# Tile 0's layer 0 on unsplit weights, between the turns of W0, in a three-layer CIN kernel

## The reference

```python
x_vec = input                                   # (512, 64, 16): batch b, fields f, embedding d
for W, b in params:                             # three layers, 128 outputs each
    z = jnp.einsum('bhd,bfd->bhfd', x_vec, input)
    z = z.reshape(B, h * f, d)                  # h*f = 4096, then 8192, 8192
    x_vec = jnp.einsum('oc,bcd->bod', W, z) + b[None, :, None]
    outs.append(x_vec.sum(axis=2))
return jnp.concatenate(outs, axis=1)            # (512, 384)
```

## Time and profile before

| | us |
|---|---|
| runs (3) | 1109.91, 1110.55, 1111.24 |
| median | 1110.55 |
| profiled execution | 1111.36 |
| its span, first to last instruction | 1109.6 |
| TensorE busy with matmuls | 1078.9 (97%) |
| VectorE busy | 863.8 (78%) |
| Pool busy | 862.1 (78%) |
| ScalarE busy | 713.5 (64%) |

### The profile page before, as it was taken

One profiled execution on the slowest core, in us unless ns is written; L12 is line 12 of the kernel. 1 busy time (PEld: TensorE's weight loads), 2 busy tenths in 40 slices (PEclk: granted clock), 3 DMA queues, 4 the chain that ended last, 5 costly groups with the idle time before them and its releaser, 6 DMA issues.

```text
span 1109.6 us, 17740 instructions
## 1 busy us (share of the span) xinstructions
PE 1078.9 (97%) x4781; PEld 808.4 (73%) x4781; DVE 863.8 (78%) x2529; ACT 713.5 (64%) x2428; POOL 862.1 (78%) x727
## 2 busy tenths in 40 slices
PE   6889999999999999999999999999999999999997
PEld 5767677777778777777778777777777877777776
DVE  5665888889894788988885698888887588888981
ACT  2566767767673676767673676766766476676771
POOL 2457897989984799897976779797988579798560
PEclk8999999999999999999999999999999999999998
DMA  7743333223241332324332142333232232321000
GB/s 280 196 101 96 74 92 79 77 55 96 50 101 39 66 84 54 97 65 86 84 67 58 45 87 82 70 93 74 77 68 64 63 69 77 79 77 41 1 23 8
DMA packets 108325, 85.87 MB, mean 77 GB/s; under 512 B 71040, under 2 KB 73824, under 8 KB 108096
## 3 DMA queue, kind: packets, MB, share of 16 engines
q1 hardware_dynamic: 106832, 78.17, 28.5%
q10 hardware_dynamic: 1392, 6.55, 1.9%
HBM read 14.75 MB, written 0.79 MB: 14 GB/s over the span
## 4 chain that ended last, share of the span: by engine, by line
PE 85%; DVE 6%; ACT 5%; issue 2%; DMA 1%; POOL 1%; ACTq 0%; DVEq 0%
PE y L881 57%; PE l L901 11%; PE l L881 7%; PE xt L992 5%; PE l2p L1004 3%; DVE acc L740 3%; ACT prod L638 2%; ACT y L627 2%; DVE acc L725 1%; DMA gram<-in_L_rec_W_dram 1%; DVE gram L824 1%; PE l L951 1%; PE l2p L981 1%; ACT x1h L536 1%; DVE bd L696 0%
## 5 line engine op out<-in xcount | busy, mean ns | idle before, releaser
L740 DVE SCALAR_TENSOR_TENSOR acc<-y,x0t,acc 128x128 f32<-128x128 f32 x1792 | 493.2, 340 | 62.6 <-PE y L881 58.2
L638 ACT ACTIVATE prod<-y,x0t 128x128 f32<-128x128 f32 x1280 | 367.7, 380 | 221.7 <-PE y L881 215.3
L881 PE MATMUL y<-w1h,x1h 128*128 128x512 f32 x1024 | 469.1, 458 | 3.9 <-DVE acc L740 3.7
L881 PE MATMUL y<-w1h,x1l 128*128 128x512 f32 x1024 | 402.7, 393 | 0.0
L881 PE MATMUL y<-w1l,x1h 128*128 128x512 f32 x1024 | 401.8, 392 | 0.0
L435 POOL TENSOR_TENSOR z<-z,xg 128x512 f32<-128x512 f32 (+2 forms) x272 | 372.2, 1373 | 24.4 <-DMA z<-xg 24.4
L445 POOL TENSOR_TENSOR pacc<-pacc,prod 128x512 f32<-128x512 f32 x192 | 253.1, 1318 | 137.2 <-ACT prod L638 137.2
L881 PEld LDWEIGHTS y<-w1h,x1h 128*128 128x128 f32 x1024 | 193.5, 189 | 108.4 <-issue 40.6
L627 ACT ACTIVATE y<-y,x0t 128x128 f32<-128x128 f32 x768 | 215.2, 349 | 75.8 <-PE y L881 75.5
L881 PEld LDWEIGHTS y<-w1l,x1h 128*128 128x128 f32 x1024 | 193.2, 189 | 59.5 <-issue 29.0
L725 DVE TENSOR_TENSOR acc<-y,acc 128x512 f32<-128x512 f32 x192 | 132.6, 691 | 131.8 <-ACT y L627 129.6
(11 more groups left out here) (92 smaller groups left out, 652.6 us busy)
## 6 DMA issues: line engine op xcount, KB each, us to landing
z<-xg SPq DMA_DIRECT2D x480, 128.0 KB, 2.4
w2t<-in_L_rec_W_dram SPq DMA_DIRECT2D x8, 512.0 KB, 9.0
gram<-in_L_rec_W_dram ACTq DMA_DIRECT2D x8, 512.0 KB, 4.7
xg<-in_r_input_dram SPq DMA_DIRECT2D x30, 128.0 KB, 3.9
z<-xg SPq DMA_DIRECT2D x32, 96.0 KB, 2.7
z<-xg SPq DMA_DIRECT2D x15, 192.0 KB
gram<-in_L_rec_W_dram ACTq DMA_DIRECT2D x1, 2048.0 KB, 9.7
out_dram<-z SPq DMA_DIRECT2D x4, 192.0 KB, 1.9
```

The lines of the kernel that those rows point to most:

```text
L638: last = nc.scalar.activation(prod[:, h % HSLOTS, k, :], y[c % YB][:, k * O:(k + 1) * O], ACT.Copy, scale=x0t[:, j, f:f + 1])
L740: ins = nc.vector.scalar_tensor_tensor(out=to, in0=of, scalar=x0t[:, j, f:f + 1], in1=b1r[:] if m == 0 else to, op0=ALU.mult, op1=ALU.add)
L881: ins = nc.tensor.matmul(to, stationary, moving, start=(first and k == 0), stop=(last and k == 2))
```

## The change

Layer 0 of tile 0 is computed on the turned weights as they are, before they are split. ScalarE copies each bank whole to SBUF first (over w0pair's part of the same step, which has been read), and TensorE multiplies four steps of tile 0 by it behind a later turn: turn 0; turn 1, steps 0 to 3; turn 2, steps 4 to 7; the left turn, steps 8 to 11; turn 3, steps 12 to 15; the left product. The order of W0's turns becomes 0, 1, 2, 4, 3, and VectorE adds the left block's pairs ahead of step 3's.

VectorE's subtractions for w0l read the whole copy in SBUF and not the bank, so the bank is free when ScalarE has read it (`wh_made`). They stand behind the one for the left block. x1l of tile 0 is computed ahead of the first two w1l. W2's first transfer waits for the subtractions, since it overwrites the whole copies. SP's W1 transfers wait for `xturned_made` (VectorE's copy of the turned rows) and not for `x_turned`, and the copies from t = 2 on for `early_turned` and not for `prep_made`. In the groups' layer 0, the split steps of group 0 wait for w0l.

```diff
             def first_front():
-                sp.wait_ge(x_turned, 1)
+                sp.wait_ge(xturned_made, 1)
...
                     if t == 2:
-                        sp.wait_ge(prep_made, W0_STEPS)
+                        sp.wait_ge(early_turned, W0_STEPS)
...
             def load_w2(k):
+                if k == 0:
+                    act.wait_ge(w0l_made, W0_STEPS - 1)
...
-            for r in range(W0_STEPS):
-                act.wait_ge(prep_made, r + 1)
+            for k, r in enumerate(W0_ORDER):
+                act.wait_ge(prep_made, k + 1)
                 if r < W0_STEPS - 1:
+                    nc.scalar.copy(whole_weights(r), y[w0_bank(r)][:]).then_inc(w0whole_made, 1)
...
             for r in range(W0_STEPS - 1):
+                if r == W0_STEPS - 2:
+                    add_pairs(w0pair_left.rearrange("p (k i) -> p k i", i=ZLAST), ...
...
-            for r in range(W0_STEPS):
-                dve.wait_ge(wh_made, r + 1)
-                part, of = weights(w0l, r, UPPER_LOWER)
+            dve.wait_ge(wh_made, W0_ORDER.index(W0_STEPS - 1) + 1)
+            part, of = weights(w0l, W0_STEPS - 1, UPPER_LOWER)
+            whole, _ = weights(w0h, W0_STEPS - 1, UPPER_LOWER)
+            nc.vector.tensor_tensor(part, of, whole.bitcast(F32), ALU.subtract).then_inc(w0left_made, 1)
+            for r in range(W0_STEPS - 1):
+                dve.wait_ge(wh_made, W0_ORDER.index(r) + 1)
+                part, of = weights(w0l, r, UPPER_LOWER, whole_weights(r))
                 whole, _ = weights(w0h, r, UPPER_LOWER)
-                nc.vector.tensor_tensor(part, of, whole.bitcast(F32), ALU.subtract).then_inc(y_used[w0_bank(r)], 1)
+                nc.vector.tensor_tensor(part, of, whole.bitcast(F32), ALU.subtract).then_inc(w0l_made, 1)
+            lower(0, FIRST)
             for k in range(W1_AHEAD):
                 w1_lower(k)
-            lower(0, FIRST)
...
+            def early_layer0(r):
+                pe.wait_ge(early_z_made, r + 1)
+                pe.wait_ge(w0whole_made, r + 1)
+                for t in range(4 * r, 4 * r + 4):
+                    nc.tensor.matmul(l0[:, EARLY], whole_weights(r)[:, (t % 4) * O:(t % 4 + 1) * O],
+                                     zfirst[r][:, t % 4, :], start=(t == 0), stop=False)
...
-            for r in range(W0_STEPS):
+            turn_w0(0)
+            for r in range(1, W0_STEPS - 2):
                 turn_w0(r)
-            early_layer0()
+                early_layer0(r - 1)
+            turn_w0(W0_STEPS - 1)
+            early_layer0(W0_STEPS - 3)
+            turn_w0(W0_STEPS - 2)
+            early_layer0(W0_STEPS - 2)
+            early_left()
             for k in range(W1_AHEAD):
                 turn_w1(k)
-            for i in range(YB):
-                pe.wait_ge(y_used[i], w0_uses(i))
+            pe.wait_ge(wh_made, W0_STEPS)
```

More of the change, by code:

```diff
@@ L206, in cin_kernel @@
         prep_made = sem("prep_made")
+        w0whole_made = sem("w0whole_made")
         wh_made = sem("wh_made")
+        w0l_made = sem("w0l_made")
+        w0left_made = sem("w0left_made")
         w2_turned = sem("w2_turned")
@@ L230, in cin_kernel @@
         y_made = sem("y_made")
-        y_used = [sem(f"y_used{i}") for i in range(YB)]
         acc_step = sem("acc_step")
@@ L248, in cin_kernel @@
         W0_STEPS = -(-ZT // 4)
+        W0_ORDER = (0, 1, 2, 4, 3)
         def w0_bank(r):
@@ L254, in pair_steps, with whole_weights, weights @@
         def pair_steps(r):
[L256 to L262, removed]
+            return 3 * min(r + 1, W0_STEPS - 1) + (1 if r < W0_STEPS - 2 else 2) if r < W0_STEPS - 1 else 3 * (W0_STEPS - 2) + 2
+        def whole_weights(r):
+            return w0pair[:, 4 * r * O:4 * (r + 1) * O]
+        def weights(to, r, rows, of=None):
             if r < W0_STEPS - 1:
@@ L266, in weights @@
                 i, step = PARTED.index(tiles[0]), tiles[-1] - tiles[0] if len(tiles) > 1 else 1
-                return to[:, i:i + len(tiles), :], y[w0_bank(r)][:].rearrange("p (t o) -> p t o", o=O)[
+                of = y[w0_bank(r)][:] if of is None else of
+                return to[:, i:i + len(tiles), :], of.rearrange("p (t o) -> p t o", o=O)[
                     :, tiles[0] % 4:tiles[-1] % 4 + 1:step, :]
@@ L827, in _ @@
             for r in range(W0_STEPS - 1):
+                if r == W0_STEPS - 2:
+                    add_pairs(w0pair_left.rearrange("p (k i) -> p k i", i=ZLAST),
+                              at(w0raw, F * half, [0, ZCOPIES], [F + 1, half]),
+                              at(w0raw, half, [0, ZCOPIES], [F + 1, half]))
                 s0, n = PAIR_SHIFTS * r, PAIR_SHIFTS
@@ L841, in _ @@
                     steps += 1
-            add_pairs(w0pair_left.rearrange("p (k i) -> p k i", i=ZLAST),
-                      at(w0raw, F * half, [0, ZCOPIES], [F + 1, half]),
-                      at(w0raw, half, [0, ZCOPIES], [F + 1, half]))
             dve.wait_ge(bias_loaded, 48)
@@ L893, in layer0 @@
                 if t in PARTED:
+                    if n == 0:
+                        pe.wait_ge(w0l_made, t // 4 + 1)
                     i = PARTED.index(t)
@@ L917, in turn_w0 @@
                 if r >= YB:
-                    pe.wait_ge(y_used[w0_bank(r)], 1)
+                    pe.wait_ge(wh_made, r - YB + 1)
                 pe.wait_ge(pair_step, pair_steps(r))
@@ L937, in turn_w1, with early_left @@
                 last.then_inc(w1_turned, 1)
[L939 to L952, removed]
+            def early_layer0(r):
[4 more added lines that the diff above has]
+                                     zfirst[r][:, t % 4, :], start=(t == 0), stop=False)
+            def early_left():
                 rows = z_rows(ZT - 1)
-                pe.wait_ge(y_used[w0_bank(W0_STEPS - 1)], w0_uses(w0_bank(W0_STEPS - 1)))
+                pe.wait_ge(w0left_made, 1)
                 pe.wait_ge(early_left_lowered, 1)
```

## The result

The changed kernel takes 1104.95 us (median of 6 runs, 1103.19 to 1107.15); the kernel before, run beside it, 1111.55 (6 runs, 1109.91 to 1112.77). The ratio is 0.9942, 95% interval 0.9926 to 0.9957: 6.4 us less (4.8 to 8.2), a small gain but clear of the noise. The forecast was 8.4 us less and 1102.2, with a range of 1100.4 to 1106.0; about 1.0 us of the distance to 1104.95 is that the first three runs of the kernel before lay lower than the later ones. The profiled execution has a span of 1102.7 us, before 1109.6.

What follows compares the result with a forecast made beforehand. The start's chain of waits before TensorE's dense stretch was taken as the room; 5.98 + 0.9 + 1.5 = 8.4 us off 1111.36 gave 1103.0, and 1102.2 for the median, range 1100.4 to 1106.0.

Steps and rivals of the forecast that it cites:

- (a): Start: W1's transfer leaves later, so W0 lands sooner and pair sums start at 10.69; bounded by 0 and 0.99 us.
- R2: Rival: W0 lands no sooner, VectorE still starts at 11.66; costs 0 to 1 us; chance within the forecast's 0.55.
- (b): Layer 0 of tile 0 on unsplit weights: 32 instructions and the left one, not 46 and one; 1.6 to 3.0 us.
- (c): Layer 0's place between W0's turns: left product ends by 22.95, not 28.93; layer 0 5.98 us earlier in all.
- R1: Rival: the clock stays low until 26 us, 2.8 us less of the sum, 1105.0; chance 0.20.
- (d): Behind layer 0: x1l ahead of W1's lower parts, TensorE resumes 2.25 us behind layer 0, not 3.13; 0.9 us.
- (e): First chunks: shorter idle time behind layer 0 keeps the clock up; 1.5 us, bounded by 0 and 1.5.
- (f): Added copies, moved subtractions and later transfers at the start: held hidden, Pool keeping about 4 us; priced 0, bounds 0 and +1.5.
- R4: Rival: slower than before, Pool's first seven products caught between later z copies and W2's earlier transfers; 1111.5; chance 0.04.
- The tail: Slow-clock stretch holding 1091 to 1094.5 us: may come out some two us shorter or longer, about +-1 us.
- R3: Rival: the clock never falls at 15.8, layer 0 at about 21.9, W1's last parts then bound; 1101.2; chance 0.15.
- R5: Rival: the gain is taken back between 36 and 130 us, by W2's landing or x's next load; 1108.5 to 1110.5; chance 0.06.

Runs made afterwards that it cites:

- d1: Changed kernel with W1's transfers held until all of W0 has landed; one run, 1105.71 us.
- a1: Changed kernel with W1's transfers released early again, by x_turned; ratio to the kernel before 0.9947.
- a2: Changed kernel with x1l behind the first two lower parts of W1 again; ratio to the kernel before 0.9962.
- b2: Kernel before with one edit, W1's transfers waiting for the copy of x's turned rows; one run, 1109.66 us.
- a4: Changed kernel with W0's turns in order 0, 1, 2, 4, 3 and layer 0's 32 instructions behind them all; ratio to the kernel before 0.9958.
- b1: Kernel before with one edit, x1l ahead of the first two lower parts of W1; ratio to the kernel before 0.9981.
- c1: Changed kernel with 36 spare turns of the identity in TensorE's holes up to W0's second turn; ratio to the kernel before 0.9938.
- b3: Kernel before with spare turns in TensorE's holes up to W0's last turn and eight behind W1's second turn; ratio to the kernel before 0.9979.
- e3: Changed kernel with W1 early, W1's first turn in the last bank's hole, spare turns, and W2's transfers at chunks 3 to 10; 1103.67 us, ratio 0.9935.
- a3: Changed kernel with layer 0 of tile 0 counting the split steps twice, 46 instructions in the new place; ratio to the kernel before 0.9946.
- c2: Changed kernel with spare turns in TensorE's holes and W1's transfers early again; median 1103.67 us, ratio to the kernel before 0.9930.
- e1: Changed kernel with W1 early and its first chunk turned and split while TensorE waits for the last bank's copy; ratio to the kernel before 0.9954.

## Why the prediction was right, and by how much each step was off

The median lies in the forecast range, and the gain is 2.0 us short of the forecast's 8.4. Half of that is term (a), 0.97 us that did not come; the other half is less than the width of the measured interval (4.8 to 8.2).

**(a), W0 sooner by 0.97 us: wrong.** It was forecast from 1.8 us less of shared transfer; the first sum started at 11.64, as before. The step that failed is that W0 "then has the DMA engines to itself longer": it had them to itself in the kernel before as well. The transfers by queue, 6.4 to 9 us (packets, MB, share of the 16 DMA engines; q10 is ScalarE's queue, with x and W0, q1 is SP's), first before, then changed:

```profile
q10 hardware_dynamic: 59, 0.97, 92.8%
q1 hardware_dynamic: 15, 0.01, 1.2%
```

```profile
q10 hardware_dynamic: 60, 0.98, 93.1%
q1 hardware_dynamic: 14, 0.01, 1.2%
```

W1's transfers stood in SP's queue from 6.35 us before and from 8.11 in the changed kernel, and from 6.4 to 9 us that queue moved 0.01 MB in both; from 9 to 11 us it moved 0.39 and 0.37 MB. Only from 11 us on, when W0 is in, does the delay of W1 show (from 11 to 12 us 0.39 MB and 0.25). d1 shows the end of W0 by itself: with nothing of W1 on its way, 10 to 11 us, W0's queue moves 0.16 MB and keeps the 16 engines 38.4% busy, so it does not want for engines. R2 was the case that came, and for its reason. (R2's price is slipped by half a microsecond in the prediction: 0 to 1 us on 1102.2 begins at 1102.2 and not at 1102.7.)

Over 14 profiles the first sum starts at 11.03 to 13.06 with W1 early (seven: 11.03, 11.66, 12.78, 12.93, 12.96, 13.05, 13.06), at 11.15 to 12.51 with W1 late (six), and at 12.11 with W1 behind W0. Most of this scatter is there before W1's first transfer is issued in any of them: until 6.2 us ScalarE's queue had moved 0.93 to 1.16 MB in the four profiles that start by 11.66 (two with W1 early, two late), and 0.70 to 0.87 MB in the other ten. What sets it is not known. Among these ten the five with W1 early start at 12.78 to 13.06 and the five with W1 late or held at 12.10 to 12.51. So when W0 is late, an early W1 seems to cost it another half microsecond. Sorted afterwards, with one profile a kernel, this is likely and not shown, and the times show nothing of it (a1 0.9947, changed 0.9942).

**(b) and (c), layer 0: right.** Forecast 12.26 us from the first sum to the left product's end (22.95 - 10.69); measured 12.05, and 12.19 to 13.30 in the other profiles with the same TensorE stream (a1, a2, d1), before 17.27 and 16.40 (b2). The clock came up at about 19.1 in the changed profile (the second block takes 1.06 us), taken as 19.2; in a1 it did so only at the third block, at 23.1, between the forecast and R1. That it fitted to 0.1 us here is luck, and so is the way to it: the prediction has the clock up at 12.3 and down again at 15.8, as before, but in the changed profile it had not come up before 19.1, for the 16 early turns take 3.82 us (before 3.46) and the first turn of W0 1.12 (before 0.66). What holds in all of them is the place of the blocks. The split of the gain: a4 puts the place, with the clock that goes with it, at 2.4 to 3.6 us; the fewer products are an estimated 1.6.

**(d), 0.9 us: right.** 0.64 in the changed kernel, where W1's lateness took 0.3 of it; 0.98 in b1, 0.95 in a1.

**(e), the clock in the first chunks, 1.5 us: 1.28** (11.83 to 10.55), and 1.38 in b1. With a resume of 3.1 us the first chunks were slow in before, a2, b2 and c1 (11.70 to 12.32), and not in b3, whose hole was filled with spare turns, but also not in d1 (10.52), whose resume was 3.33. c1 and d1 have nearly the same TensorE rows there (holes of 0.82 and 0.92 us, and of 1.00 and 0.91), and the clock fell in one of them only. So a long hole does not always cost it, and this term is partly a matter of chance in each execution.

**(f), what was held to be hidden.** W1 was to be complete at 21 to 22.3 us; it was at 23.8, late enough for the 0.17 us hole. The misreading is in (a): from the rate at 20.0 to 20.5 us the last two parts were taken as nearly in. In the kernel before the last part was issued at 11.4 and landed 10.5 us later, at 21.9; with 1.8 us more that is 23.7. Pool's cover was to be 4 us and was nothing. The 4.28 us wait is where W2's first transfers (27.1, 28.3 and 31.1 us) meet the copies; in e3, with W2 later, the copies come one every 1.3 us. So z copies are held up as in R4, but Pool's first sum comes no later by it, within 0.05 us, in any profile ("to Pool" is 10.55 in the changed kernel and 10.52 in d1, the two with no cover left). Where "to Pool" is longer, 10.80 to 10.94 in a3, c2 and e1, Pool has 0.9 to 3.9 us of cover. There a late product of Pool runs beside VectorE's first zl subtraction, which takes 0.83 to 0.97 us and not 0.55, and TensorE waits for it 1.33 to 1.46 us and not 1.02 to 1.05. That is 0.3 to 0.4 us, by the effect described in the last section.

**The tail.** All profiles have a slow stretch of 6.8 us there but a4, where it is 3.4 us; its rest is 0.9 to 1.6 us shorter, the size I had put down.

Sum by the profile: 0.0 + 5.2 + 0.6 + 1.3 = 7.1 us, less 0.3 in the rest, is the 6.9 us between the spans. The forecast less the term (a) was 7.4.

R3 did not come either (layer 0 ended at 23.7, not 21.9), and its limit, W1, was felt all the same. Nor did R5: the 7.1 us of Pool's first sum are 6.9 us in the span. R1 did not come. The page TensorE: Matmul & The Clock Gate of the Trainium skill, Part 4, says that the full clock does not engage for transposes, which do not count as busy in the same way. c1 speaks against it for these transposes: with nothing but turns up to 16.9 us, its first turn of W0 took 0.66 us for four and the block behind the second 1.06, where the changed kernel needed 1.12 and 1.91. The few early turns by themselves are no sure way to it: they end at the full clock in the kernel before (274 ns each), and not in the changed kernel (1.12 us for the four turns behind them).

## What to carry to other kernels

Work whose operands are ready belongs in the holes of the engine that ends the stage, and there it also keeps the clock up: here that, and one reordered subtraction, gave nearly all of 6.4 us, and either can be sized from the rows of before. A transfer is worth delaying only where the rows show that it moves bytes while the other one is on its way; the waits of the engines don't tell that, nor does the rate of all queues together, but the bytes of each queue in that stretch do. When a transfer is in is read from its issue and its time to landing, not from a rate that has gone down. When the start of a kernel gets shorter, count again the cover of everything that fed its end (here Pool's products, from 12 us to nothing).

## What the runs showed of the hardware that I had not expected

**A subtraction in SBUF beside Pool.** The change lets w0l's subtraction read the whole copy in SBUF and not the bank in PSUM. While Pool is idle that costs nothing. Beside Pool's products most of them take twice as long and more. VectorE's subtractions (ns min/median/max) in the changed kernel, where they end before Pool starts, and in a1, where Pool starts at 23.24:

```profile
L868 DVE TENSOR_TENSOR w0l<-gram,w0h x4: 293/418/425, 21.1 to 23.1; 128x256 fp32r<-128x256 f32 x3, 128x128 fp32r<-128x128 f32 x1
```

```profile
L868 DVE TENSOR_TENSOR w0l<-gram,w0h x4: 410/1050/1210, 23.5 to 25.9; 128x256 fp32r<-128x256 f32 x3, 128x128 fp32r<-128x128 f32 x1
```

It is not every one: the 410 ns one in a1 starts at 25.57, just ahead of a product of Pool at 25.63, and then it is Pool's product that is longer (1.24 us and not 1.0); in a2 the last takes 0.29 us at 24.78 and Pool's product at 24.85 takes 1.10. It looks as if the one that comes second waits; that is read from these two cases.

An earlier W1 brings Pool's work forward, onto these subtractions. In a1 that cost TensorE nothing, as the first w1l still waits for ScalarE (0.29 us) and the resume is 2.18; in e1 it took the gain. It is the cost in (f) that I put at nothing without its cover named. It is not only in the start: zl, with both operands in SBUF too, takes 0.55 us while Pool is idle (32.72 in the changed kernel) and 0.96 beside Pool (39.46). That the bank in PSUM as an operand would have spared w0l this was not tried; w0left, which is still read from the bank, keeps its 283 ns beside Pool in e1. The Trainium skill (GPSIMD Engine Reference, 1. Specifications) says that Pool shares its SBUF interfaces with VectorE, with contention for VectorE's instructions that have two SBUF inputs; the runs agree, and w1l, with one operand in PSUM, kept its 691 ns beside Pool.

**The granted clock can be unknown at the start.** The row of the changed kernel for 15.8 to 19 us gives 1.00, while its block at 16.86 runs at 0.213 us an instruction:

```profile
15.80:19.00 3.20, 3.05 (x15) 3.05 (x16) 2.99 (x7) 1.73 (x7) 0.00 (x0) 1.00 1.02 379
```

In such a stretch the durations of like instructions tell the level (1.91 us or 1.06 for eight), and not the column; the mean clock of the two spans (0.991 and 0.997) is not to be compared either.
